# New instruction orders for an adaLN transformer block on one core: statistics ahead of the silu, the scale's first copy ahead of a low part

## The reference

```python
x = L0_attn_x                                    # (4, 1024, 1024)
mod = (_silu(L0_c) @ L0_wmod).reshape(4, 6, 1, -1)
sa, ca, ga, sb, cb, gb = (mod[:, i] for i in range(6))
...
h = _layernorm(x, axis=-1) * (1 + ca) + sa
x = x + ga * _L0_attn_ref(h, Wqkv, bqkv, Wo, bo)   # q, k, v of 256 columns, softmax over 1024 keys
h = _layernorm(x, axis=-1) * (1 + cb) + sb
x = x + gb * _L0_ffn_ref(h, weight, bias, lora_A, lora_B, starts)
```

## Time and profile before

| what | us |
| --- | --- |
| median of 3 runs (lowest, highest) | 1036.54 (1036.51, 1036.72) |
| the profiled execution's own time | 1036.71 |
| its span in the trace | 1034.9 |
| PE busy | 1007.2 |
| DVE busy, ACT busy, POOL busy | 660.2, 312.3, 235.7 |

### The profile page before, as it was taken

The page is one execution under the profiler, slowest core; times in us unless marked ns, Lnnn a source line. Parts: engine busy times, 40 slices in busy tenths (PEclk is TensorE's granted clock), DMA queues, the critical chain, the costliest instruction groups (busy, mean ns, idle before and its releaser), DMA issues.

```text
span 1034.9 us, 13028 instructions
## 1 busy us (share of the span) xinstructions
PE 1007.2 (97%) x5213; PEld 830.1 (80%) x5213; DVE 660.2 (64%) x830; ACT 312.3 (30%) x468; POOL 235.7 (23%) x181
## 2 busy tenths in 40 slices
PE   4899999999999999999999999999999999999996
PEld 3767678889888888889898788888888888888885
DVE  5966766588543685543858547867685677477722
ACT  2423333122331222422253423412441433143200
POOL 0000000423202122020312033343333323142411
PEclk9999999999999999999999999999999999999998
DMA  9988764865104353033344146646562755374321
GB/s 364 391 325 304 250 241 135 281 235 188 59 1 161 125 198 128 1 112 133 142 151 142 49 153 233 220 146 224 185 222 84 247 178 183 128 231 157 114 78 65
DMA packets 54428, 180.23 MB, mean 174 GB/s; under 512 B 5872, under 2 KB 6432, under 8 KB 54368
## 3 DMA queue, kind: packets, MB, share of 16 engines
q1 hardware_dynamic: 45152, 146.33, 41.0%
q0 software_dynamic: 9072, 33.03, 8.6%
q10 hardware_dynamic: 144, 0.03, 0.0%
HBM read 145.72 MB, written 33.64 MB: 173 GB/s over the span
## 4 chain that ended last, share of the span: by engine, by line
PE 94%; SPq 2%; DMA 2%; DVE 1%; issue 0%; ACT 0%; DVEq 0%; ACTq 0%
PE pairA L1420 8%; PE pairA L1421 8%; PE pairA L1422 8%; PE pairD L1420 7%; PE pairD L1421 7%; PE pairD L1422 7%; PE pairC L1420 7%; PE pairC L1421 7%; PE pairC L1422 7%; PE pairB L1420 6%; PE pairB L1422 6%; PE pairB L1421 6%; DMA w_raw<-in_wqkv 2%; SPq L819 1%; PE pairB L1617 1%; PE pairB L1552 1%
## 5 line engine op out<-in xcount | busy, mean ns | idle before, releaser
L956 POOL TENSOR_TENSOR res<-res,row_bc 128x1024 f32<-128x1024 f32 x32 | 84.2, 2640 | 85.4 <-DMA res<-x_dram 76.7
L943 POOL TENSOR_TENSOR xr<-xr,row_bc 128x1024 f32<-128x1024 f32 x32 | 81.2, 2544 | 92.8 <-DMA xr<-in_x 92.3
L1420 PE MATMUL pairD<-w_hi,h_hi 128*128 128x256 f32 (+1 forms) x256 | 87.0, 340 | 0.0
L1421 PE MATMUL pairD<-w_lo,h_hi 128*128 128x256 f32 (+1 forms) x256 | 86.6, 338 | 0.0
L1422 PE MATMUL pairD<-w_hi,h_lo 128*128 128x256 f32 (+1 forms) x256 | 86.3, 337 | 0.0
L948 POOL DMA_DIRECT2D x_dram<-xr x32 | 18.1, 567 | 258.6 <-DVE xr L1326 258.6
L1420 PE MATMUL pairC<-w_hi,h_hi 128*128 128x512 f32 (+1 forms) x192 | 72.3, 377 | 3.2 <-DVE h_lo L1249 2.7
L1421 PE MATMUL pairC<-w_lo,h_hi 128*128 128x512 f32 (+1 forms) x192 | 71.9, 375 | 0.0
L1422 PE MATMUL pairC<-w_hi,h_lo 128*128 128x512 f32 (+1 forms) x192 | 71.7, 373 | 0.0
L1117 ACT ACTIVATE w_hi<-w_sum 128x1024 fp32r<-128x1024 f32 x32 | 33.9, 1060 | 119.6 <-DVE w_sum L1370 119.3
L1421 PE MATMUL pairA<-w_lo,h_hi 128*128 128x256 f32 (+1 forms) x192 | 65.0, 338 | 0.0
(11 more groups left out here) (352 smaller groups left out, 2543.0 us busy)
## 6 DMA issues: line engine op xcount, KB each, us to landing
wm<-in_wmod SPq DMA_DIRECT2D x40, 512.0 KB, 5.4
xr<-in_x SPq DMA_DIRECT2D x34, 512.0 KB, 4.2
z_cols<-in_x_cols SPq DMA_DIRECT2D x32, 512.0 KB, 5.9
x_dram<-xr POOLq DMA_DIRECT2D x32, 512.0 KB, 3.2
xs<-x_dram SPq DMA_DIRECT2D x32, 512.0 KB, 4.5
w2t<-in_w2t SPq DMA_DIRECT2D x32, 512.0 KB, 4.5
res<-x_dram SPq DMA_DIRECT2D x32, 512.0 KB, 6.3
out_y<-res POOLq DMA_DIRECT2D x31, 512.0 KB, 3.3
```

Source lines behind the costliest of these rows:

```text
L943: nc.gpsimd.tensor_tensor(xt, xt, row_bc[:, :], ALU.add).then_inc(residual_made, 1)
L956: nc.gpsimd.tensor_tensor(rt, rt, row, ALU.add).then_inc(residual2_made, 1)
L1420: nc.tensor.matmul(out, left[0], right[0], start=first, stop=False, skip_group_check=True)
L1421: nc.tensor.matmul(out, left[0], right[1], start=False, stop=False, skip_group_check=True)
```

## The change

All five tables are replaced; no step is added or removed, and the code that the steps run stays. After the change every line of the code stands three lines higher. On DVE the four ST of the first 512 rows stand ahead of SI, and MM0(0) ahead of WQL(1,0); MM0(1) then stands behind WQL(1,1), which stood behind it. V0(3) and K0(3) go behind Q(0,0,0) on PE, the first two scores go ahead of V(0,1,0), and further steps move by a few places, to the end. The heads of the tables, and the places that the prediction speaks of:

```diff
@@ DVE_ORDER @@
-    ("SI", (), None), ("ST", (0, 0), None), ("ST", (0, 1), None), ("ST", (0, 2), None), ("ST", (0, 3), None),
+    ("ST", (0, 0), None), ("ST", (0, 1), None), ("ST", (0, 2), None), ("ST", (0, 3), None), ("SI", (), None),
@@ PE_ORDER @@
-    ("BCP", (1,), "A", ("BCM", 0)), ("BCM", (1,), "A", None), ("V0", (3,), "C", None),
+    ("BCP", (1,), "B", ("M0", 3)), ("M", (1, 0), "A", ("BCM", 0)), ("BCM", (1,), "B", None),
+    ("M", (1, 1), "A", None), ("Q", (0, 0, 0), "B", ("BCM", 1)), ("M", (1, 2), "A", None), ("V0", (3,), "C", None),
```

More of the change, by code:

```diff
@@ L392 @@
     ("LN", 1, 0), ("Lwm", 1, 4), ("Lwm", 1, 5), ("Lwm", 1, 6), ("Lwm", 1, 7), ("LN", 1, 1), ("Lwm", 2, 0),
-    ("Lwm", 2, 1), ("Lwm", 2, 2), ("Lwm", 2, 3), ("LN", 1, 2), ("LT", 1, 0, 0), ("LT", 1, 0, 1), ("LT", 1, 0, 2),
-    ("LT", 1, 0, 3), ("Lwm", 2, 4), ("Lwm", 2, 5), ("LN", 1, 3), ("Lwm", 2, 6), ("Lwm", 2, 7), ("LN", 1, 4),
-    ("Lwm", 3, 0), ("Lwm", 3, 1), ("SW", 1, 0), ("Lwm", 3, 2), ("Lwm", 3, 3), ("LN", 1, 5), ("LBC", 1, 0),
-    ("Lwm", 3, 4), ("Lwm", 3, 5), ("Lwm", 3, 6), ("Lwm", 3, 7), ("LN", 1, 6), ("Lwm", 4, 0), ("Lwm", 4, 1),
-    ("LN", 1, 7), ("RS_", 0), ("Lwm", 4, 2), ("Lwm", 4, 3), ("LN", 2, 0), ("Lwm", 4, 4), ("RS_", 1), ("Lwm", 4, 5),
-    ("SW", 1, 1), ("Lwm", 4, 6), ("Lwm", 4, 7), ("LN", 2, 1), ("LBC", 1, 1), ("Lwm", 5, 0), ("Lwm", 5, 1),
-    ("Lwm", 5, 2), ("Lwm", 5, 3), ("LN", 2, 2), ("Lwm", 5, 4), ("Lwm", 5, 5), ("LN", 2, 3), ("Lwm", 5, 6),
[14 rows of a table removed]
-    ("LW2", 1, 0), ("LRES", 0, 1, 0, 0), ("LW2", 1, 1), ("LRES", 0, 1, 0, 1), ("LRES", 0, 0, 1, 0),
[1 row of a table removed]
+    ("Lwm", 2, 1), ("Lwm", 2, 2), ("Lwm", 2, 3), ("LN", 1, 2), ("Lwm", 2, 4), ("Lwm", 2, 5), ("Lwm", 2, 6),
+    ("Lwm", 2, 7), ("LN", 1, 3), ("LT", 1, 0, 0), ("LT", 1, 0, 1), ("LT", 1, 0, 2), ("LT", 1, 0, 3), ("LN", 1, 4),
+    ("Lwm", 3, 0), ("Lwm", 3, 1), ("Lwm", 3, 2), ("Lwm", 3, 3), ("LN", 1, 5), ("SW", 1, 0), ("Lwm", 3, 4),
+    ("Lwm", 3, 5), ("LBC", 1, 0), ("RS_", 0), ("Lwm", 3, 6), ("LN", 1, 6), ("Lwm", 3, 7), ("Lwm", 4, 0),
+    ("Lwm", 4, 1), ("LN", 1, 7), ("RS_", 1), ("Lwm", 4, 2), ("Lwm", 4, 3), ("LN", 2, 0), ("Lwm", 4, 4),
+    ("Lwm", 4, 5), ("Lwm", 4, 6), ("Lwm", 4, 7), ("SW", 1, 1), ("LN", 2, 1), ("LBC", 1, 1), ("Lwm", 5, 0),
+    ("Lwm", 5, 1), ("LN", 2, 2), ("Lwm", 5, 2), ("Lwm", 5, 3), ("Lwm", 5, 4), ("Lwm", 5, 5), ("LN", 2, 3),
[14 rows of a table added]
+    ("LRES", 0, 1, 0, 0), ("LW2", 1, 0), ("LW2", 1, 1), ("LRES", 0, 1, 0, 1), ("LRES", 0, 0, 1, 0),
[1 row of a table added]
     ("LRES", 0, 1, 1, 1), ("LRES", 1, 0, 0, 0), ("LRES", 1, 0, 0, 1), ("LW2", 1, 5), ("LR2", 1), ("LX", 6),
[3 rows of a table removed]
[3 rows of a table added]
     ("LRES", 2, 0, 0, 1), ("LR2", 2), ("LX", 10), ("LG2", 2), ("LW2", 2, 6), ("LW2", 2, 7), ("LX", 11),
[4 rows of a table removed]
[2 rows of a table added]
+    ("LRES", 2, 1, 1, 0), ("LRES", 2, 1, 1, 1), ("LRES", 3, 0, 0, 0), ("LRES", 3, 0, 0, 1), ("LR2", 3), ("LX", 14),
+    ("LG2", 3), ("LX", 15), ("LW2", 3, 6), ("LRES", 3, 1, 0, 0), ("LW2", 3, 7), ("LRES", 3, 1, 0, 1),
     ("LRES", 3, 0, 1, 0), ("LRES", 3, 0, 1, 1), ("LRES", 3, 1, 1, 0), ("LRES", 3, 1, 1, 1),
```

## The result

The changed kernel takes 1045.17 us (median, 1044.5 to 1046.31), the kernel before 1036.62 in the same comparison: a ratio of 1.0081, with a 95% interval of 1.0069 to 1.0093. So it is slower by 0.8%, small but clear of the noise. I had forecast 1036.5 and at most 1039.0. The profiled execution took 1044.5 us, with a span of 1042.7.

A forecast was written before the change was run, and what follows sets the result against it. PE, busy 1007.2 of 1034.9 us, was taken as the bound, so an order could gain only its idle time. The start's loss and the middle's gain summed to +1.4 - 1.4 = 0.0: 1036.5 us, range 1035.2 to 1039.0.

The forecast's parts named there:

- Statistics ahead of the silu: At the start, PE's first matmul (BCM) moves from 11.85 to about 10.6, a gain so far of 1.2 us.
- MM0(0) ahead of WQL(1,0): At the start, the copy comes earlier and K0(0) moves from 20.30 to 18.3, gaining 2.0 us at this place.
- MM0(1) behind WQL(1,1): At the start, V0(0) starts at 27.1, 1.8 us later, leaving PE about 1.4 us behind.
- V0(3) behind M(1,1) and Q(0,0,0): At the start, Q(0,0,0) waits for a load landing at 49.0, starts at 49.5; the same work ends 1.1 us late.
- M(1,2): Behind Q(0,0,0), PE waits 0.3 us for its second tile, bounds 0 and 1.0; the start then costs 1.4 us.
- PP and W in batch 3: In the middle, between 590 and 628, three PE waits vanish: 1.4 us gained, bounds 0 and 1.4.
- The rest of the first batch: After the start, PE never waits over 543 us and producers are ready in time: 0, bounds 0 and +3.
- The first rival: Q(0,1,0) waits for EX(0,0) if a row load lands late: 0.3 us, or 1039.4 us at 97.5; chance 0.11.
- signs of being wrong: V0(0) near 25, Q(0,0,0) before 49, or PE waits between 60 and 590 or after 628.
- End: The last rows of all tables are the same but for pairs: 0.
- Rival 4: An NM pair runs beside a POOL addition and T waits, up to 4.2 us, taken at half: 1038.6; chance 0.07.

The follow-up runs named there:

- v03: Kernel before, with V0(3) moved behind M(1,1) and Q(0,0,0), and the copies that read it (VH, VL) moved back too: 1038.12 us, ratio 1.0013.
- hyb_tail: Changed kernel's tables up to about 330 us, tables of the kernel before from there on: 1038.25 us, ratio 1.0016 to the kernel before.
- abc: Changed kernel with both moves of c_both, TLA behind EX(3,3) on ACT, and O(2,6) ahead of T(1,0) on PE: 1037.97 us, ratio 1.0012.
- c_both: Changed kernel with RS2(3) ahead of RA(3,6) on POOL and NM(3) ahead of X1(3,6) on DVE: 1039.81 us, ratio 1.0032.
- hyb_best: Tables of before up to about 330 us, the changed kernel's behind, with NM(3), RS2(3) and NM(1) earlier and TLA later: 1035.39 us, ratio 0.9986.
- ra_short: Changed kernel with POOL's additions RA(2,6) and RA(2,7) cut to the first 16 of 1024 columns: 1042.63 us, ratio 1.0062.
- c_pool: Changed kernel with only RS2(3) moved ahead of RA(3,6) on POOL: 1045.43 us, ratio 1.0087.
- c_dve: Changed kernel with only NM(3) moved ahead of X1(3,6) on DVE: 1041.24 us, ratio 1.0046.

## Why the prediction was wrong

The start went as predicted, step by step. The timeline of the changed kernel, PE:

```profile
10.30 2.04 PE L1484 MATMUL pairA<-consts,stat 128*128 128x128 f32 x8 [10.30 <-DVE stat L1221]
...
18.86 1.21 PE L1564 MATMUL pairD<-h_hi,w_hi 128*128 128x512 f32 x4
...
27.11 0.58 PE L1417 MATMUL pairC<-w_hi,h_hi 128*128 128x256 f32 x1 [0.39 <-DVE modT L1144]
...
49.75 0.50 PE L1417 MATMUL pairB<-h_hi,w_hi 128*128 128x512 f32 x1
...
56.56 0.39 PE L1417 MATMUL pairC<-w_hi,h_hi 128*128 128x256 f32 x1
```

- *Statistics ahead of the silu*: BCM at 10.30, said 10.6. *MM0(0) ahead of WQL(1,0)*: K0(0) at 18.86, said 18.3. *MM0(1) behind WQL(1,1)*: V0(0) at 27.11, said 27.1.
- *V0(3) behind M(1,1) and Q(0,0,0)*: Q(0,0,0) at 49.75, said 49.5; V0(3) at 56.56, said 56. *M(1,2)*: it does not wait, where I took 0.3. The start costs 1.2 to 1.3 us, said 1.4; v03 and hyb_tail confirm its cause and size. That the sum fits so well is partly luck, since the 1.1 came out a little larger and the 0.3 as nothing.
- *PP and W in batch 3*: by the account 2.0 us come back from 578 to 639, said 1.4. PP's wait and the fourth W's are gone. The third, O(3,6) for WS(0,3), which I had taken as gained too, is still there, at 629.9 instead of 627.4: it left the window up to 628, not the trace.
- *The rest of the first batch*, taken as 0: right up to 530: no PE wait, and the distance to the kernel before stays at 1.1 to 1.3. The first rival (the first exponential) did not occur. But the step covered everything up to 590, and in it lie the waits at 536 (1.6 us) and 571 (1.75 us). This step failed. My sentence that each producer was ready before PE asks, the closest with 1.3 us, was false for NM(1) and for EX(3,2). PE waits between 60 and 590 and behind 628 are two of the signs of being wrong that I had named.
- *End*, taken as 0 because the last rows are the same: I had worked out nothing between 628 and those rows, and 5.3 us were lost at 644. This step failed too, and it had the larger part.
- *Rival 4* names the mechanism, and got a chance of 0.07 and a price of 2.1 us. It occurred twice. At 536 it cost 1.6, near its price. At 644 it cost more, because the queue in front of NM(3) added to its longer duration (X1(3,6), and behind it a load until 639.8), and because a stretch at the lower clock followed the 3.6 us of idle PE. The prediction had neither in its sum. I also argued that the trace of before has such pairs without a wait behind them; that says how much slack those places had, and the change's places have another.
- Two slips that decided nothing: in the first rival, 4.0 us of cover behind 95.3 put the need at 99.3, not 99.1, and a landing at 97.5 adds 2.9 us to the wait of 0.3 that was there already, 3.2 in all. And K0(3), which the section on the change has going behind Q(0,0,0), stood behind it before.

The sum put right, by the table above: 1.1 of start as it stands at 530, 1.65 at 536, 1.75 at 571, 1.5 back and 0.5 more by 639, 5.3 at 644, together 7.8, by which the two spans differ.

The error was one of reading. I followed PE, DVE and ACT by durations, and POOL and the row loads not at all, though both tables print the reversal: before, NM(3) stood ahead of X1(3,6) on DVE and RS2(3) ahead of RA(3,6) on POOL; now they stand behind.

## What to carry to other kernels

Where many orders change at once, look on each engine for steps that moved behind one that waits for a transfer or another engine (X1(3,6) behind its row tile, an exponential behind TLA), and ask what stands behind it. Do that for the engines that are never busy too: POOL, at 22%, had a part in the largest loss here twice over, as the addition that X1(3,6) waited for and as the one that ran beside NM(3). And repair a late result at its producer, since covering its wait on the reader's engine moved much of it to the next reader (abc), while starting the producer earlier removed it (c_both, hyb_best).

## What was unexpected of the hardware

- Two DVE operations of 0.81 us take 5.34 us together beside two additions of POOL, and 1.53 when these are cut to 16 columns. The prediction had weighed up to 4.2 us for such a pair; it was 3.8. What it had not seen is where a caught pair ends: 0.55 us behind the end of the addition beside it, at both places (537.51 behind 536.96, and 647.39 behind 646.84). So what it costs here goes by when POOL is done.
- In the changed kernel a PE idle for 3.5 us is followed by about 3 us at the lower clock, in which the matmuls step by 0.43 us instead of 0.23; this cost some 1.7 us more. It is so in ra_short's trace as well (idle 3.5 us, then 0.50 from 649 to 651), but not in c_pool's behind 3.06 us. Behind the idle 1.48 us at 536 and the 1.26 us at 571 the granted clock stays at 1.00. At the start, where PE is idle in pieces of 0.3 to 1.5 us from 21 to 27, it stands at 0.50 from 27 to 30. The view by windows of the changed kernel there:

```profile
25.00:26.00 1.00, 0.00 (x0) 0.00 (x0) 0.24 (x1) 0.99 (x2) 0.00 (x0) 1.00 1.03 410
...
28.00:29.00 1.00, 1.00 (x7) 1.00 (x7) 1.00 (x2) 0.49 (x1) 0.00 (x0) 0.50 1.03 410
```

- Sometimes moving one step changes an operation's duration much more than its start: in c_dve NM(3) starts 0.5 us earlier and ends 2.9 earlier.
